# Attention on one core: y in groups of four key tiles instead of two, with six probability buffers and another order of loads

## The reference

```python
c6 = jax.nn.silu(c) @ Wc + bc
sh_msa, sc_msa, g_msa, sh_mlp, sc_mlp, g_mlp = jnp.split(c6, 6, axis=-1)
xm = _modulate(_ln(x), sh_msa, sc_msa)
q = (xm @ Wq + bq).reshape(B, S, NH, DH); k = ...; v = ...
q = q / DH
w = jax.nn.softmax(jnp.einsum('bqhc,bkhc->bhqk', q, k), axis=-1)
y = jnp.einsum('bhqk,bkhc->bqhc', w, v).reshape(B, S, H)
x = x + g_msa[:, None, :] * (y @ Wo + bo)
xm2 = _modulate(_ln(x), sh_mlp, sc_mlp)
h = jax.nn.gelu(xm2 @ W1 + b1, approximate=False)
x = x + g_mlp[:, None, :] * (h @ W2 + b2)
```

## Time and profile before

| | |
|---|---|
| time, median of 3 runs | 2948.42 us (2947.97 to 2952.46) |
| the profiled execution | 2950.05 us |
| its span, first to last instruction | 2948.2 us |
| mean granted clock of PE | 0.982 |
| busy: PE, DVE, POOL, ACT | 2863.9, 2033.7, 1998.3, 1339.6 us |

### The profile page before, as it was taken

One profiled execution on the slowest core, in us unless ns is written; L12 is line 12 of the kernel. 1 busy time (PEld: TensorE's weight loads), 2 busy tenths in 40 slices (PEclk: granted clock), 3 DMA queues, 4 the chain that ended last, 5 costly groups with the idle time before them and its releaser, 6 DMA issues. The chain is left out here.

```text
span 2948.2 us, 40747 instructions
## 1 busy us (share of the span) xinstructions
PE 2863.9 (97%) x14713; PEld 1815.9 (62%) x14713; DVE 2033.7 (69%) x3384; ACT 1339.6 (45%) x2535; POOL 1998.3 (68%) x1012
## 2 busy tenths in 40 slices
PE   7999999999999999999999999998699999999998
PEld 5777555555555555555555555552587777777777
DVE  5444587777777777777777777773757757766764
ACT  2222156666666666666666666665111111111111
POOL 1000079999999999999999999996554545545453
PEclk9999789999999999999999999999799999999999
DMA  6444832422414314323324324202201101100000
GB/s 229 171 172 164 212 69 57 97 66 66 110 43 99 90 34 106 79 61 90 72 65 97 81 52 98 69 24 97 104 1 44 43 1 44 43 21 23 29 15 15
DMA packets 152766, 225.19 MB, mean 76 GB/s; under 512 B 31804, under 2 KB 48760, under 8 KB 152568
## 3 DMA queue, kind: packets, MB, share of 16 engines
q1 hardware_dynamic: 123036, 204.81, 25.6%
q10 hardware_dynamic: 29532, 17.79, 2.1%
HBM read 162.30 MB, written 58.97 MB: 75 GB/s over the span
## 5 line engine op out<-in xcount | busy, mean ns | idle before, releaser
L839 DVE TENSOR_REDUCE part_max<-m_bank 128x1 f32<-128x512 f32 x2048 | 1252.1, 679 | 395.0 <-PE m_bank L925 394.9
L820 ACT ACTIVATE probs<-s_bank 128x512 f32<-128x512 f32 x2048 | 1035.3, 626 | 241.7 <-PE s_bank L939 237.6
L939 PE MATMUL s_bank<-qs,ks 97*128 97x512 f32 x2048 | 847.0, 415 | 2.5 <-ACT probs L820 2.2
L722 POOL TENSOR_TENSOR low_sum<-probs 128x1024 f32<-128x1024 f32 x248 | 589.2, 2387 | 121.4 <-ACT probs L820 121.2
L737 POOL TENSOR_TENSOR high_sum<-high_sum,probs 128x1024 f32<-128x1024 f32 x256 | 608.4, 2376 | 42.5 <-ACT probs L820 5.7
L939 PEld LDWEIGHTS s_bank<-qs,ks 97*128 97x128 f32 x2048 | 385.9, 189 | 342.1 <-issue 211.2
L949 PE MATMUL y_bank<-probs,vs 128*32 128x512 f32 x4096 | 497.3, 603 | 0.0
L1315 ACT ACTIVATE h<-up_bank,vecs 128x512 f32<-128x512 f32 x128 | 88.2, 689 | 634.9 <-PE up_bank L1340 634.9
L730 POOL TENSOR_TENSOR high_sum<-probs 128x1024 f32<-128x1024 f32 x128 | 308.0, 2406 | 13.0 <-ACT probs L820 13.0
L949 PEld LDWEIGHTS y_bank<-probs,vs 128*32 128x32 f32 x4096 | 107.5, 109 | 243.7 <-issue 133.6
L1139 POOL TENSOR_TENSOR w_lo<-space_plain,w_hi 128x512 fp32r<-128x512 f32 x64 | 87.3, 1365 | 206.1 <-DVE w_hi L1224 206.1
(11 more groups left out here) (141 smaller groups left out, 3797.4 us busy)
## 6 DMA issues: line engine op xcount, KB each, us to landing
qs<-q_parts SPq DMA_DIRECT2D x96, 256.0 KB, 5.6
ks<-k_parts SPq DMA_DIRECT2D x96, 256.0 KB, 5.1
q_parts<-qk_out SPq DMA_DIRECT2D x32, 512.0 KB, 3.4
k_parts<-qk_out SPq DMA_DIRECT2D x32, 512.0 KB, 3.4
xb<-in_x SPq DMA_DIRECT2D x12, 1024.0 KB, 7.5
space_parts<-q_parts SPq DMA_DIRECT2D x48, 256.0 KB, 4.9
space_parts<-k_parts SPq DMA_DIRECT2D x48, 256.0 KB, 4.6
late_parts<-k_parts SPq DMA_DIRECT2D x48, 256.0 KB, 4.5
```

What stands on the lines that cost most here:

```text
L722: pool.tensor_tensor(low_sum[:, (2 * c + half) % 4, :, :], probs[:, first % RING, hs, :], probs[:, (first + 1) % RING, hs, :], ALU.add).th ...
L820: act.activation(probs[:, tile % RING, h, :], s_bank[(HPG * tile + h) % 3][:, :], ACT.Exp).then_inc(p_done, 1)
L839: v.tensor_reduce(part_max[:, i % 2, hs, c:c + 1], m_bank[ring.bank["max", i, n]][:, :], AX.X, ALU.max).then_inc(m_taken, 1)
L939: pe.matmul(s_bank[n % 3][:, :], ks[:, h, t * P:(t + 1) * P], qs[i % 2][:, h, :], start=True, stop=True).then_inc(s_done, 1)
```

## The change

The diff does the following.

- PE does y after every fourth tile instead of every second, and then for four tiles: the last one of the quad before (4b - 1) and the first three of the quad that it has just scored. The sums of the quad before stand behind these; only in the first quad of an iteration (t = 3) they stand between the first and the others, where y's bank changes over to the new iteration.
- The ring of banks is worked out for that order; `due_quad` goes.
- `probs` holds six tiles instead of five.
- ACT takes y at t = 3 before the third head, instead of at the beginning of t = 2.
- SP loads the values of chunk c one step later, and the row of maxima before the values of chunk 2.
- The scratch space for DMA descriptors is halved, which makes room for the sixth buffer.

```diff
-N_BLOCKS = N_TILES // 2
-RING = 5
+RING = 6
-def due_quad(b):
-    return (b - 3) // 2 if b >= 3 and b % 2 == 1 else None
@@ class MaxRing
-                b, within = divmod(N_SC * i + s, 2 * HPG)
-                if within == 2 * HPG - 1 and due_quad(b) is not None and due_quad(b) <= LAST_QUAD:
-                    uses.append(("sum", due_quad(b)))
+                b, within = divmod(N_SC * i + s, 4 * HPG)
+                if within == 4 * HPG - 1 and 0 <= b - 1 <= LAST_QUAD:
+                    uses.append(("sum", b - 1))
@@ SP, iteration(i)
                         load_ks(group + 1, c)
-                        sp.wait_ge(av_done, NKT * i + CHUNK * (c + 1))
-                        load_v(group + 1, c)
+                        if c:
+                            sp.wait_ge(av_done, NKT * i + CHUNK * c)
+                            load_v(group + 1, c - 1)
                 if i + 1 < N_IT:
                     load_row(i + 1)
                 if qt == BPB - 1 and more_groups:
-                    c = BPB - 1
+                    sp.wait_ge(av_done, NKT * i + CHUNK * (BPB - 1))
+                    load_v(group + 1, BPB - 2)
                     sp.wait_ge(s_done, N_SC * (i + 1))
-                    load_ks(group + 1, c)
+                    load_ks(group + 1, BPB - 1)
                     sp.wait_ge(av_done, NKT * (i + 1))
-                    load_v(group + 1, c)
+                    load_v(group + 1, BPB - 1)
@@ ACT
-                    if t == 2 and i:
-                        take_y(i - 1)
                     if tile >= 8 and tile % 4 == 0 and (tile - 8) // 4 < LAST_QUAD:
                         take_sum((tile - 8) // 4)
                     for h in range(HPG):
+                        if t == 3 and h == 2 and i:
+                            take_y(i - 1)
@@ PE
-                    if t % 2 == 1:
-                        b = (NKT * i + t) // 2
+                    if t % 4 == 3:
+                        b = (NKT * i + t) // 4
                         if b:
-                            times_v(2 * b - 2)
-                            times_v(2 * b - 1)
-                        if due_quad(b) is not None:
-                            sums(due_quad(b))
-            times_v(N_TILES - 2)
+                            times_v(4 * b - 1)
+                            if t == 3:
+                                sums(b - 1)
+                        for tile in range(4 * b, 4 * b + 3):
+                            times_v(tile)
+                        if t > 3:
+                            sums(b - 1)
             times_v(N_TILES - 1)
             sums(N_QUADS - 1)
@@ kernel
-    nc = bacc.Bacc("TRN2", target_bir_lowering=False, num_devices=1)
+    nc = bacc.Bacc("TRN2", target_bir_lowering=False, num_devices=1, dynamic_dma_scratch_size=8192)
```

## The result

The changed kernel takes 3104.22 us (median of 4 runs, 3094.91 to 3108.29) against 2949.73 us before: a ratio of 1.052, 95% interval 1.049 to 1.055. The forecast was 3042 us, in a range of 3000 to 3075. The direction was right; the loss is 155 us where 94 were forecast. Lines of the code have moved: L921, L935 and L945 are what L925, L939 and L949 were, L816 is the exponential, L835 the reduction.

A forecast was written before the change was run, and what follows sets the result against it. TensorE was taken to set the pace, with DVE holding back the new phases of 16. Quad terms of 17.1, 47.1, 17.7 and 10.2 plus 2 us gave +94 on 2950.05, less 1.63: 3042 us, range 3000 to 3075.

The forecast's parts named there:

- The edges saved: Half the groups of y go: each quad loses one exit (0.14) and one pair of edges (0.19), 0.33 us.
- DVE paces a phase of 16: Plain quad: product 16 waits for DVE's reductions, 0.60 us apart; y starts at 8.55 us, +0.57 us net.
- The quad with the row: Fourth quad of an iteration: DVE's negation and row cast delay reductions 0.44 us; y at 8.99, +0.34 us net.
- The first and the third quad: Plain quads of an iteration, paced by DVE in a phase of 16: +0.57 us each.
- The issues in mid-phase: Second quad, t=5: ACT's four DMA issues delay exponential 9; y at 9.53 us, +1.55 us net.
- Rival A: Second quad: ACT's issues cost nothing, overlapping with queued exponentials; 3011 us, chance 0.12.
- Ring, take_y, scratch: Six buffers with POOL hidden, take_y at t=3 covered by the group, halved DMA scratch: cost 0 each.
- The row ahead of v 2: SP's load order: row moved ahead costs 0; left behind v 2, PE loses a few us at eight iterations.
- The first and the last iteration: First: long phase already in quad 0, +0.57 us each in quads 1 and 2; last: ACT paces, 2 us.
- Sum: Whole kernel: terms of plain, second and row quads and the last iteration total +94 us, forecast 3042 us.
- the term of the second quad: Second quads with ACT's four issues in mid-phase: 30 x 1.55 + 0.57 = 47.1 us in all.
- rival C: TensorE's clock falls to 1.2 GHz in one or two groups of each of 31 iterations: 3095 to 3147 us, chance 0.08.

The follow-up runs named there:

- the halved reductions: Changed kernel with the four issues at t=7, and each maximum taken over only the first 256 of its 512 columns: 2938.56 us.
- the filled wait: Changed kernel plus five superfluous copies of one product of the maxima just before TensorE's wait in the second quad: 3038.79 us.

## Why the prediction was right and wrong

- *The edges saved (0.33 us a quad):* right. Groups after are 5.29 and 4.43 us, the lengths worked out.
- *DVE paces a phase of 16 (8.55):* right, 8.52; that this is the cause, the halved reductions show (7.81).
- *The quad with the row (8.99):* 8.96.
- *The first and the third quad (+0.57):* +0.50 and +0.39. The forecast took all phases before as 3.92, but the second one of the third quad lost 0.11 us to the load of inv at t=10 (4.05 in the median), and the other plain phases were 3.94. DVE's pace hides that now.
- *The issues in mid-phase (9.53, +1.55 a second quad):* right in length, 9.56 where the clock held. Rival A, that they hide, is refuted.
- *Ring, take_y, scratch:* no cost, as forecast; of these the ring was tried by itself.
- *The row ahead of v 2:* the forecast held that the old order would cost PE a few us at eight iterations (they are seven, since the last group loads no next one). It costs about 1 us in all, and that in one place, a wait of 1.11 us ahead of iteration 16. That the group of y, twice as long now, covers the row otherwise fits, but wasn't tried apart.
- *The first and the last iteration (about 1 and 2):* 2.0 and 3.4, small misses.
- *Sum:* 3042 forecast for a clock that holds; 3038.79 measured once the wait was filled. That is 87 us over its kernel before where 94 were forecast: the first and third quads are under their terms, the last iteration is over.

The step that failed is the term of the second quad, 30 x 1.55, which took a clock that holds. It came to 30 x 1.55 + 72 us. The forecast priced ACT's delay by its length alone and left its effect on the clock to rival C, given 0.08, since PE "stays over 90% busy", pointing to DVE-paced products that ran at full clock. Those were the wrong rows to argue from. DVE's pacing draws each pair of products out from 0.467 to 0.60 us; the delay is one wait of 1.3 us inside the phase, and in iterations 1 to 29 of the trace before PE has no wait over 0.15 us. What PE loses is 1.95 us in the phase and 1.07 in the group, 3.0 in 22 of the 25 falls and 1.6 to 2.0 in the three others, twice the 1.55 of the delay itself. That the wait is what sets the clock off, and not DVE's pacing, the filled wait shows: the pacing is the same there, and no clock falls. The rival's own price, one half-speed group in each iteration, gave 3095; 3104 was measured. That it is so near is in part luck: it has 53 us for the clock where 72 were measured, and 94 for the rest where it was 86. In the Trainium skill, "TensorE: Matmul & The Clock Gate", section on HAM oscillation, waits of 3 to 5 us for data in each turn of a loop of matmuls throttle the engine again every time. The wait here is shorter, 1.3 us, and the granted clock is 0.66 in the 10 us behind it all the same, though not every time.

## What to carry to other kernels

When an edit lengthens a stretch between two rests, compare the pace of each engine that reads its results with the producer's (0.60 and 0.49 against 0.467 us here), and count how far the buffers carry: an average of 76% busy said nothing, four banks said product 8 to 10. Then look what else was hidden in the rests that are gone; here four small transfers' issues. And price a wait that falls on TensorE twice, by its length and by what it does to the clock, and break it up or move part of it elsewhere.

## What was not expected of the hardware

- One wait of 1.3 us, in a phase in which TensorE otherwise works without a gap, is followed by up to 7 us at 1.2 GHz in 13 to 25 of 30 cases; one of 1.5 us near the end of a short phase, with the issues moved in the kernel before, in 10 of 30; waits of 0.76 us in none of 30. Waits of 1.5 to 3.5 us in third quads, in the two kernels with the issues at t=7, did it in 7 of 7. Between 0.76 and 1.3 us nothing was measured.
- Redundant matmuls in that wait, 1.17 us of them, made the kernel 65 us faster than the same kernel without.
- The issue of four transfers holds back ACT's next exponential until 0.18 us after the last issue has ended (1014.88 to 1015.06), though the first one starts before exponential 8 does.
